# Payload rows moved by SP's DMA queue instead of a ScalarE copy, in a fused attention and mixture-of-experts kernel

## What is computed

```python
h = layer_norm(x)                                  # x: 512 x 32 tokens of 128 channels, f32
q, k, v = h @ Wq, h @ Wk, h @ Wv                   # 4 heads of 32
x = x + (softmax(causal(q k^T * C**-0.5)) v) @ Wo + bo
nx = layer_norm(x)
noisy = nx @ Wr + br + noise * softplus(nx @ Wn + bn)
top 2 of 8 experts, gates = softmax over the two
expert_e(nx) = relu(nx @ W1[e] + b1[e]) @ W2[e] + b2[e]     # hidden 512
out = x + sum of gate * expert, but x alone where sigmoid(nx @ Wsk + bsk) > 0.5
```

## Time and profile before

| | |
|---|---|
| runs, median of 3 (us) | 761.32 |
| the profiled execution (us) | 763.97 |
| its span, first to last instruction (us) | 762.2 |
| busy in the span: PE, DVE, ACT, POOL | 541.4, 556.7, 503.0, 425.9 us |
| PE's mean granted clock | 0.873 of full speed |
| the loop over groups | from the start to about 436 us |
| the expert phase | from about 441 to 667 us |

### The profile page before, as it was taken

One profiled execution on the slowest core, in us unless ns is written; L12 is line 12 of the kernel. 1 busy time (PEld: TensorE's weight loads), 2 busy tenths in 40 slices (PEclk: granted clock), 3 DMA queues, 4 the chain that ended last, 5 costly groups with the idle time before them and its releaser, 6 DMA issues.

```text
span 762.2 us, 17132 instructions
## 1 busy us (share of the span) xinstructions
PE 541.4 (71%) x4556; PEld 409.9 (54%) x4556; DVE 556.7 (73%) x2097; ACT 503.0 (66%) x1113; POOL 425.9 (56%) x440
## 2 busy tenths in 40 slices
PE   2576888988988888988963079999999999700000
PEld 1345665666666665666652057777777777600000
DVE  4456788788878778887873447778777778529997
ACT  3647788898888788889863068888888888400000
POOL 9630677676766767767677605666666666440000
PEclk9888999999999999999986579999999999855555
DMA  8874345545545545555457477666676666139998
GB/s 230 271 249 160 100 133 149 148 131 142 148 127 145 150 115 149 153 133 142 120 143 139 176 292 233 223 229 229 236 245 249 226 227 228 60 112 311 325 335 260
DMA packets 139234, 144.32 MB, mean 189 GB/s; under 512 B 25250, under 2 KB 109315, under 8 KB 139168
## 3 DMA queue, kind: packets, MB, share of 16 engines
q1 hardware_dynamic: 108704, 115.18, 49.8%
q0 software_dynamic: 13568, 19.96, 8.0%
q10 hardware_dynamic: 16896, 8.39, 3.7%
HBM read 73.86 MB, written 62.78 MB: 179 GB/s over the span
## 4 chain that ended last, share of the span: by engine, by line
PE 35%; ACT 18%; issue 16%; DVE 12%; POOL 8%; DMA 5%; SPq 3%; DVEq 2%; POOLq 1%; ACTq 0%
ACT z L736 7%; PE ps L569 7%; POOL expert_rows L1223 6%; PE ps L705 4%; PE ps L706 4%; PE ps L707 4%; PE ps L693 4%; PE ps L694 4%; PE ps L695 4%; DVE z L1142 3%; ACT hT L759 2%; DVE z L1147 2%; PE ps L648 2%; ACT pay L823 1%; ACT kT L789 1%
## 5 line engine op out<-in xcount | busy, mean ns | idle before, releaser
L1223 POOL DMA_INDIRECT expert_rows<-pay,rows_of x256 | 253.1, 989 | 124.9 <-issue 74.5
L1243 POOL DMA_INDIRECT expert_results<-z,words x128 | 136.9, 1069 | 105.3 <-DVE z L1109 74.0
L736 ACT ACTIVATE z<-xres,shift,rstd 128x128 f32<-128x128 f32 x256 | 105.1, 483 | 29.7 <-DVE shift L972 29.7
L1123 DVE TENSOR_TENSOR hlo<-h,hhi 128x512 fp32r<-128x512 f32 x128 | 90.0, 703 | 45.4 <-ACT hhi L865 44.3
L863 ACT ACTIVATE h<-ps,w1x 128x512 f32<-128x512 f32 x128 | 88.2, 689 | 35.2 <-PE ps L695 31.7
L865 ACT ACTIVATE hhi<-ps,w1x 128x512 fp32r<-128x512 f32 x128 | 87.2, 682 | 0.0
L569 PE MATMUL ps<-ident,z 128*128 128x128 f32 x256 | 43.8, 298 | 42.2 <-ACT z L736 42.2
L705 PE MATMUL ps<-hhi,w2x 128*128 128x512 f32 x128 | 57.3, 448 | 4.2 <-issue 4.2
L569 PEld LDWEIGHTS ps<-ident,z 128*128 128x128 f32 x256 | 31.7, 157 | 45.2 <-ACT z L736 35.2
L931 DVE BATCH_NORM_STATS2 stats<-xres 128x6 f32<-128x128 f32 x256 | 52.7, 278 | 3.8 <-DMA xres<-in_r_x 3.7
L919 DVE TENSOR_TENSOR xres<-ps,xres 128x512 f32<-128x512 f32 x32 | 22.1, 692 | 44.7 <-PE ps L648 43.6
(11 more groups left out here) (155 smaller groups left out, 1304.7 us busy)
## 6 DMA issues: line engine op xcount, KB each, us to landing
w1x<-split_weights SPq DMA_DIRECT2D x33, 514.0 KB, 3.7
w2x<-split_weights SPq DMA_DIRECT2D x33, 512.5 KB
expert_results<-zeros SPq DMA_DIRECT2D x32, 512.0 KB
pay<-expert_rows SPq DMA_DIRECT2D x33, 264.0 KB, 3.5
xres<-in_r_x SPq DMA_DIRECT2D x32, 256.0 KB, 6.1
hhi<-kT SPq DMA_DIRECT2D x128, 64.0 KB
hlo<-pT SPq DMA_DIRECT2D x128, 64.0 KB
hhi<-expert_results SPq DMA_DIRECT2D x16, 512.0 KB, 5.4
```

Of the source, the lines that this page charges most:

```text
L736: m = nc.scalar.activation(z[:, j:j + 1], tile(xres, n, j), ACT.Identity, bias=shift[:, which, j:j + 1], scale=rstd[:, which, j:j + 1])
L1123: ev.tensor_tensor(hlo[:, c], h32[:, c % 2], hhi[:, c].bitcast(F32), ALU.subtract).then_inc(s_h_lo, 1)
L1223: g.indirect_dma_start(rows, bass.IndirectOffsetOnAxis(ap=rows_of[:, odd, k * J + j:k * J + j + 1], axis=0), pay[:, odd, k, j, :], None, b ...
L1243: g.indirect_dma_start(results, bass.IndirectOffsetOnAxis(ap=words[:, slot, j:j + 1], axis=0), yrow[slot][:, j, :], None, bounds_check=K * ...
```

## The change

Five edits:

1. ACT's copy of z2 into the payload (line 823) is taken out. SP moves the rows with two SBUF-to-SBUF DMAs of 256 KB a group, `load_pay(n)`, in its step t = n+3, between `spread_p` and `load_x`. It waits for z2 of the group and for the sends of group n-2.
2. ACT's copy of the token word goes from step n+2 to step n+3, with its wait for the sends.
3. POOL's sends wait for the two DMAs in place of the copy.
4. ACT's z2 waits, besides, until the DMAs that read the buffer two groups before have landed.
5. On ACT, oT of group t-1 moves ahead of kT of t+1 and z2 of t-2. On PE, WO of t-1 moves ahead of the transposes of z2 of t-2.

```diff
+            def load_pay(n, par):
+                wait(sp, s_z2, n + 1)
+                wait(sp, sent[par], pair(n, par, SENT))
+                if n == 0:
+                    sp.wait_ge(s_pay_zeroed, 1)
+                for k in range(K):
+                    sp.dma_start(pay[:, par, k, :, 0:C], z2[:, par]).then_inc(pay_in[par], 16)
+
             def step(t, par):
                 odd = 1 - par
                 n = t - 1
                 if live(n):
                     spread_p(n, odd)
+                n = t - 3
+                if live(n):
+                    load_pay(n, odd)
                 n = t + 3
                 if live(n) and not (isinstance(n, int) and n < EARLY):
                     load_x(n, odd)
...
-                n = t - 2
-                if live(n):
-                    wait(act, sent[par], pair(n, par, SENT))
-                    if isinstance(n, int) and n == 0:
-                        act.wait_ge(s_pay_zeroed, 1)
-                        act.wait_ge(s_tokens, 1)
-                    nc.scalar.activation(pay_u[:, par, :, :, C], token[:, bass.ds(n, 1)].rearrange("p a k j -> p (a k) j"),
-                                         ACT.Copy).then_inc(s_word_made, 1)
-                    nc.scalar.activation(pay[:, par, :, :, 0:C], z2[:, par].unsqueeze(1).to_broadcast([P, K, J, C]),
-                                         ACT.Copy).then_inc(s_pay_made, 1)
...
                 n = t - 3
                 if live(n):
+                    wait(act, sent[odd], pair(n, odd, SENT))
+                    if isinstance(n, int) and n == 0:
+                        act.wait_ge(s_pay_zeroed, 1)
+                        act.wait_ge(s_tokens, 1)
+                    nc.scalar.activation(pay_u[:, odd, :, :, C], token[:, bass.ds(n, 1)].rearrange("p a k j -> p (a k) j"),
+                                         ACT.Copy).then_inc(s_word_made, 1)
...
                                 (s_word_made, n + 1),
-                                (s_pay_made, n + 1))
+                                (pay_in[odd], pair(n, odd, PAY) + PAY))
```

More of the change, by code:

```diff
@@ L279, in build @@
         s_tokens = sem("tokens")
-        s_pay_made = sem("pay_made")
+        s_pay_in0 = sem("pay_in0")
+        s_pay_in1 = sem("pay_in1")
         s_word_made = sem("word_made")
@@ L333, in build @@
         s_f_out3 = sem("f_out3")
+        pay_in = [s_pay_in0, s_pay_in1]
         x_in, sent = [s_x_in0, s_x_in1], [s_sent0, s_sent1]
@@ L350, in build @@
         BD = 16 * H
+        PAY = 16 * K
         EARLY = len(s_x_early)
@@ L632, in step @@
                     m.then_inc(s_rank_made, 1)
-                n = t - 2
-                if live(n):
-                    pe.wait_ge(s_z2, n + 1)
-                    transposes(ps[:, T_BANK, :], z2[:, par], s_z2T_made)
                 n = t - 1
@@ L650, in step @@
                     m.then_inc(s_wo_made, 1)
+                n = t - 2
+                if live(n):
+                    pe.wait_ge(s_z2, n + 1)
+                    transposes(ps[:, T_BANK, :], z2[:, par], s_z2T_made)
                 n = t - 2
@@ L785, in step @@
                     nc.scalar.activation(probs[:], sc_m[:], ACT.Exp, scale=SCALE).then_inc(s_exp_made, 1)
+                n = t - 1
+                if live(n):
+                    act.wait_ge(s_o_made, n + 1)
+                    wait(act, s_wo_made, n)
+                    nc.scalar.activation(oT[:].rearrange("c j b t -> c (j b t)"), ps[:, O_BANK, :],
+                                         ACT.Copy).then_inc(s_oT_made, 1)
                 n = t + 1
@@ L793, in step @@
                     wait(act, s_z2T_made, n - 1)
+                    wait(act, pay_in[par], pair(n, par, PAY))
                     norm_rows(z2[:, par], 1, n).then_inc(s_z2, 1)
[L795 to L800, removed]
                 n = t - 2
```

## The result

The changed kernel takes 776.02 us, the median of 4 runs (771.1 to 777.8), against 761.28 us for the kernel before (760.82 to 762.22): 14.7 us slower. The ratio on record is 1.0164, with a 95% interval of 1.0139 to 1.019. The two medians alone divide to 1.0194, a little above that interval; the ratio puts the loss at 12.5 us (10.6 to 14.5). 774 us were predicted, with a range of 765 to 780. The profiled execution took 777.8 us, its span is 776.0, PE's mean granted clock 0.866.

A forecast was written before the change was run, and what follows sets the result against it. The prediction took a cycle of waits, no full engine, to pace the steady loop, and POOL's sends to end its last stage. 15.9 us of uncovered SP work less 3 us gained gives 761.3 + 12.9, said as 774 us, range 765 to 780.

The forecast's parts named there:

- The block at the end: Behind the loop: SP's wait for group 29's sends holds up its late work; first expert load 15.9 us late before G.
- G: The loop's net gain, 3.6 + 2.9 - 2 - 1.5 = 3 us, taken off the lateness of the first expert load.
- tail: SP's late work from zeros to first expert load; allowed to be 4 us less to 1 more than summed.
- The step: Steady loop: the cycle over PE's logits and nabs sets 10.75 us against 10.9, saving 3.6 us over some 26 steps.
- The copy is worth almost nothing: ACT's payload copy of 1.05 us a step covered PE's logits; the change gains only 0.14 us a step.
- The wait for the sends on ACT: ACT's waits for POOL's sends in the loop, 3.7 us, fall away; 2.9 us gained.
- Losses: 2 us at the start.: Loop start: kT now stands behind oT's wait for PE, delaying SP's spreads and weight stores; 2 us lost (0 to 5).
- 0.25 us in each of 6 such steps, 1.5 us: Lower-clock loop steps: late logits no longer partly recovered through log_var's slack; 1.5 us lost.
- `load_pay` in the steady loop: hidden by 2 us, price 0.: SP's two row issues fit its 4.7 us of idleness; data lands by 232.3, needed about 234.4, so no cost.
- Rival C: SP's longer round delays its spreads; 30 steps lose 0.5 us each, G = -12, 789 us; chance 10%.
- A: ACT's relief counts in full, POOL sets a 10.3 us step; G = 19, 758 us; chance 5%.
- B: SP's work behind the loop stays covered; first load starts behind POOL's last send, 758 us; chance 3%.

The follow-up runs named there:

- e1: The kernel before plus one SP wait, for group 29's sends, ahead of its late zeros; 777.79 us, ratio 1.0164.
- f1: The changed kernel with SP's late zeros, biases and blanks put between its last three payload-row moves; 762.29 us, ratio 0.999.
- e4: The kernel before without ACT's copy of the rows into the payload and without the wait for it; 762.89 us, ratio 0.9989.
- e3: The kernel before with only the new order of oT and WO, payload copy still on ACT; 763.23 us, ratio 0.9984.
- e2c: Control of e2: the kernel before with SP's late zeros, biases and blanks spread over loop steps 6 to 24; 763.06 us, ratio 0.9999.
- e2: The changed kernel with SP's late zeros, biases and blanks spread over loop steps 6 to 24; 770.34 us, ratio 1.0095.
- g2: f1 with the five late zero blocks issued behind the rows of group 29 instead of ahead; 764.1 us, ratio 1.0002.
- f2: f1 with ACT's token-word copy and its wait for the sends moved to the step's start; 760.38 us, ratio 0.9985.
- g1: f2 with the five late zero blocks issued behind the rows of group 29 instead of ahead; 762.26 us, ratio 0.9984.
- f4: The changed kernel without load_pay's DMAs and the waits for them, payload rows staying zero; 755.91 us, ratio 0.9911.
- f3: f1 with the old order of oT, z2 and WO, rows still moved by SP; 763.65 us, ratio 1.0024.
- g3: g1 with the old order of oT and WO, behind z2 and the transposes; 766.66 us, ratio 1.0042.

## Why the prediction was right

**The block at the end** carries the result, and holds step by step. The last send of group 29 ended at 412.30, the zeros started at 414.94 (417.1 less G of 3 is 414.1 by the prediction's sum), and from the zeros to the first load it took 36.68 us (37.2 by the sum). G as POOL shows it is 2.25 (group 29's last send at 413.57 before and 411.32 after). 15.9 less 0.5 for the shorter tail less 2.25 gives 13.15, against 13.20 in the profile. The rest of the 14.7 is 0.6 us behind the first load and 0.9 by which the two profiled executions lie unlike above their medians. e1 shows the cause alone (13.6 us), f1 shows it undone (14.4 us). The Trainium skill ("DMA: Bandwidth & Descriptors", section "Anatomy of one DMA") says that the wait is held on the issuing sequencer; e1's single row, 21.3 us of SPq with everything behind it that much later, agrees.

**The step.** 10.75 us were worked out over the logits, and 10.75 to 10.76 stand in the rows, with the wait at nabs and none at log_var, as foretold. "The copy is worth almost nothing" holds in the old order, in e4. It isn't the whole of it: the new order alone makes the step 10.98 us (e3), so behind the new order the copy's removal is worth 0.23 us a step, and the two parts of the change don't simply add. The Trainium skill's rule to optimize the busiest engine ("Perfetto Trace Analysis", section "Identifying the Most-Contended Engine") names ACT in this loop. It states no time; if ACT's busy time were what counts, the copy would be worth 34 us, and e4 measured 1.3.

**The wait for the sends on ACT** is gone: between 100 and 380 us ACT has no such wait in the profile after. That this is worth 2.9 us stays the prediction's estimate; no run has it alone.

**G was right in size by luck.** 3 us were forecast and 2.25 came out, but three of the terms are off and a fourth was missing, and their errors cancel:

- *"Losses: 2 us at the start."* 3.2 us by these two profiles, and 1.5 to 6 by all that have run the same instructions up to there: nabs of one and the same step stands at 80.29 before, 80.69 in e2c and 81.67 in e1, and at 83.49 after, 83.16 in e2, 85.41 in g2 and 86.15 in f1. oT waited 3.77 us in one step ahead of it, where before it waited 0.22:

```profile
76.53 0.60 ACT L804 ACTIVATE oT<-ps 128x512 f32<-128x512 f32 x1 [3.77 <-PE ps L622]
...
83.49 0.20 ACT L760 ACTIVATE nabs<-ps 128x32 f32<-128x32 f32 x1 [0.61 <-PE ps L675]
```

- *"0.25 us in each of 6 such steps, 1.5 us"* for the lower clock. The sign looks wrong. From that nabs to rows_of of group 28 the kernel before takes 311.2 us (to 391.53) and the one after 302.9 (to 386.37): 8.4 us less. With 3.6 for the shorter steps and 2.9 for the waits, 1.9 are left, which the clock would have gained and not lost. The profile after has two low-clock steps in that part of the loop and the kernel before seven.
- *Missing: where the token word stands.* By rows_of of group 26 the loop was 5.5 us ahead (365.32 against 370.77), by POOL's first send of that group only 3.1:

```profile
371.57 0.98 POOL L1223 DMA_INDIRECT expert_rows<-pay,rows_of  x1 [1.88 <-DVE rows_of L1032]
```

```profile
368.48 0.98 POOL L1234 DMA_INDIRECT expert_rows<-pay,rows_of  x1 [0.77 <-issue]
```

Before, POOL started 0.80 us behind rows_of, and after, 3.16, since it waits for the word. From there on the kernel before sends nearly back to back, and the lead isn't won again: 2.6 us at group 28. The prediction followed the sends' wait for the rows and forgot the other edit of the same group, the word put late in step n+3. f2 and g1 price it at 1.9 and 1.8 us.
- *"`load_pay` in the steady loop: hidden by 2 us, price 0."* For the length of a single step this is right: 10.75. As a price it is wrong. f4 against f1 gives 6.4 us for the rows' moves as a whole, of which some 3 are POOL's pause in the drain, and e2 shows that the changed kernel has no slack left in SP's round. It went unnoticed in the sum because the block at the end covers what they cost there. Rival C's mechanism, late kT, is seen weakly: 5.1 us of waits in the changed kernel, but 4.3 in f4, which moves no rows. A, B and C as forecast fall, at a step of 10.75 and a first load at 451.62.

One slip of the prediction's arithmetic did no harm: G from -1 to 8 and a tail from 4 less to 1 more make 765 to 779, not 766 to 778.

What stays open: how the loss at the start divides between the rows' DMAs and the order of oT and kT (the order alone has it in e3, at 85.93, but f4 with the new order and no rows stands at 82.06, and f3 with the rows and the old order at 76.41); whether the rows or the new order took the slack that e2 wanted; which finer interleaving would spare POOL its pause in the drain (a zero block or a few biases between two row moves was not tried); and why the new order keeps the clock up. The best of the kernels that compute everything, f2, g1 and e3, are some 0.15% below the kernel before, with intervals that hold 1.0.

## What to carry to other kernels

Before a wait goes into an engine that issues DMAs, list what is queued behind it and until when that work is covered: one wait of 21 us in an idle-looking queue cost 13.6 us, and the same instructions in another order cost nothing. When an engine's work is taken away, first ask which other cycle it was covering: here 1.05 us a step off ACT bought nothing, as PE's logits ended only 0.2 us before it did, and 0.23 us a step once another edit had put it on the cycle. And when a consumer waits for several producers, follow each that the change moves, not only the one that the change is about; slack that a change takes from a queue may show only when the next edit wants it.

## What was not expected of the hardware

The granted clock went with the order of the same work. Between 90 and 372 us PE's clock fell from 2.4 to 1.2 GHz for one short stretch 7 times in the profile before, and 7, 7, 8, 6 and 8 times in e1, e2c, e4, f3 and g3, which all have WO behind the transposes. With WO ahead of them it was 2, 2, 1, 0, 0, 1, 0 and 0 times, in the profile after and in e2, e3, f1, f2, g1, g2 and f4 (one profile each). Three us inside such a stretch, and three behind it, in the kernel before:

```profile
135.00:138.00 3.00, 3.00 (x16) 2.94 (x15) 2.25 (x9) 1.90 (x7) 2.24 (x3) 0.50 0.53 132
138.50:141.50 3.00, 3.00 (x41) 1.56 (x44) 1.89 (x11) 2.03 (x7) 2.39 (x3) 1.00 0.93 276
```

PE is busy throughout both; the granted clock is 0.50 in the first and 1.00 in the second. PE's pauses in a step differ between the orders: in the old one a pause of 1.00 us stands ahead of the transposes, in the new one two of 0.40 and 0.87, apart from each other. These pauses stand in nearly every step and the clock falls in few. That they are the cause is a guess from the two orders; only the counts are shown.
